# Routed feed-forward network in items of up to 512 rows, with gate and up sums in banks of their own

## Chip, core and metric

The kernel runs on one core of one Trainium2 chip, as one program of several stages that follow each other with a barrier between them. The metric is the device time of one execution in microseconds (us); lower is better. The median of three runs of the kernel before is 2126.97 us (2122.52 to 2127.93).

## What is computed

Two layers over 2048 rows of 512 values. The change touches the feed-forward network of the first layer, in which each row goes to one of two experts:

```
logits = x @ gate_w.T
sel = argmax(softmax(logits)); top_w = probability of sel
g = einsum('td,efd->etf', x, w_gate)      # 2 experts, 2048 hidden features
u = einsum('td,efd->etf', x, w_up)
h = silu(g) * u
y = einsum('etf,edf->etd', h, w_down)
out = einsum('etd,te->td', y, onehot * top_w)
```

The kernel sorts the rows by expert and computes for each row its own expert alone. Every fp32 product is made of three matmuls on split operands (high x high, high x low, low x high; PASSES in the code), so every operand is held as a high part (a rounded copy) and a low part (the difference).

## The kernel before

The function is routed_ffn_stage. The 2048 sorted rows and 128 spare ones are 17 tiles of 128 rows. The weights of one 128-feature slice of an expert are one `w` buffer of 1536 columns: four chunks of 256 (128 gate, 128 up) and 512 of down. The 16 slices (RG) are 16 passes over all 17 tiles; two passes are one turn of a hardware loop, and the first and last two stand outside of it. In a pass, five `w` buffers serve four blocks of 4, 2, 1 and 1 pairs of tiles (RBLOCKS) and the single last tile, since each block belongs to one expert that is known only at run time.

The unit of work is a step: one pair of tiles, 256 rows, nine steps in a pass (eight pairs, then the single tile). In a step:

- TensorE (`hidden_pair`, L745) sums gate and up of the pair into the two halves of one PSUM bank `hidden`: 2 x 4 chunks x 3 passes = 24 matmuls of 256 columns. Then come the down products of the pair before (`down`, L766): 2 tiles x 3 = 6 matmuls of 512 columns into two `y` banks. The single tile takes 12 matmuls of 256 columns (L754), 3 down matmuls and one transpose of `h32_single` (L790).
- ScalarE makes the silu of the gate half (L658), then the high part of h (L666).
- VectorE multiplies up by silu into the PSUM tile `h32` (L703), makes the low part of h (L706), and adds the two `y` banks of the pair before to `rows` (L692, a copy at L690 in the first pass).

The queues run in program order. TensorE waits for the low part of h before down (`s_h`), for the addition that frees the `y` bank (`s_yadd`), and for the weights of a block (`s_w`). A weight buffer is filled (`filled`) by a DMA of SyncE's queue into one of two `raw` buffers, a high copy on ScalarE (L642) and a subtraction on GpSimd (L621); ScalarE's copies of the five buffers are queued behind the high parts of steps 5, 7, 8, 0 and 1. The DMA of a buffer waits until the buffer two before it is finished.

In the first pass the rows come in as well: TensorE turns a tile (`turn_x`, L734, four transposes), ScalarE writes the high part (L646), VectorE the low part (L678). Tiles 0 to 3 are turned ahead of the steps, in four banks; the others go through one bank `x` one after the other, each turn waiting for the low part of the tile before (`s_x`). Two tiles enter in each step, one after the hidden sums and one after down, and they are those of two steps later (LEAD = 2).

Of the kernel before, what the change touches and what calls it, by code (L numbers as in the profile page):

```python
# [11 lines left out]
P = 128  # L12
D = 512
# [464 lines left out]
def routed_ffn_stage(nc, w_dram, xs_dram, ys_dram, ident_dram, keep):  # L478
# [10 lines left out]
    def halves(n):  # L489

        return RT * (n // RU) + 2 * (n % RU)

    with ExitStack() as ctx:
# [14 lines left out]
        enter_banks = [yb[t // 2][t % 2][:].rearrange("p (c r) -> p c r", c=KC) for t in range(4)]  # L508
# [20 lines left out]
        def bank_of(t):  # L529

            return enter_banks[t] if t < 2 * LEAD else turned[:]

# [7 lines left out]
        LEAD = 2  # L540

        def walk(i, first, step):

            for j in range(2):
                for u in range(RU):
                    n = RU * j + u
                    entering = (2 * (u + LEAD), 2 * (u + LEAD) + 1) if first and j == 0 else ()
                    step(2 * RU * i + n, 2 * RT * i, n, j, u, first and n == 0, [t for t in entering if t < RT])

        def filled(i, j, u, last, fill):  # L550
# [3 lines left out]
            if u in (5, 7, 8) and not (last and j == 1):  # L554
                fill(i, RB * (j + 1) + (5, 7, 8).index(u), False)
# [61 lines left out]
        def _(pool):  # L617
# [10 lines left out]
            def body(i, first, last):  # L628
                for j in range(2):
                    for u in range(RU):  # L630
                        filled(i, j, u, last, fill)
# [3 lines left out]
        def _(act):  # L635
# [13 lines left out]
            for t in range(2 * LEAD):  # L649
                x_high(t)  # L650

            def body(i, first, last):
                def step(k, k0, n, j, u, start, entering):
                    cols = slice(0, PR if u < RP else P)
                    act.wait_ge(s_hid, k + 1)
# [7 lines left out]
                    if not isinstance(k, int) or k >= 2:  # L663
                        act.wait_ge(s_y, k0 + halves(n - 1))
                    src = hp[:, n % 2, :] if u < RP else turned[:, 0, :]
# [2613 lines left out]
```

## Time and profile before

| | before |
|---|---|
| median of three runs | 2126.97 us |
| the profiled execution: its own time | 2123.35 us |
| the profiled execution: span of the trace | 2121.6 us |
| TensorE matmuls busy | 1803.0 us (85%), 10016 instructions |
| VectorE / ScalarE / GpSimd busy | 1231.4 / 848.3 / 1032.3 us |
| mean granted TensorE clock | 0.92 |
| the routed stage's steps on TensorE | about 100 to 703 us of the span |

Busy time is the time in which an engine has an instruction under way. Matmuls overlap, so their cost is read from start to start, not from their durations. A row of the timeline gives start, duration, engine, line, operation, output <- inputs, shapes, and in brackets the engine's idle time before it with what ended it. A row with a count higher than 1 merges neighbours. The granted clock is a share of full speed: 1.00 is 2.4 GHz, 0.50 is 1.2 GHz.

### The profile page before, as it was taken

The page shows a single profiled execution, that of the slowest core. Times are in us where ns is not written, and L with a number is a line of the kernel's source. Part 1 is how long each engine was busy: PE and PEld are TensorE (multiplying, and loading weights), DVE is VectorE, ACT ScalarE, POOL GpSimd, SP SyncE. Part 2 cuts the span into 40 slices and gives each one's busy share as a digit, 9 for nine tenths or more (in the row PEclk, how much of TensorE's full clock was granted, in tenths as well). Part 3 has the DMA queues.
Part 4 walks back from the last instruction along what each step waited for, and adds up shares of the span by engine and source line. Part 5 has one row for each costly group of instructions (what it writes and reads, how often), then busy time and mean ns, then how long its engine had stood idle before and what let it go on. Part 6 is the DMA issues. An engine that isn't in the chain of part 4 may idle for free. (4 is left out here: it accounts for less than half of the span.)

```text
span 2121.6 us, 29604 instructions
## 1 busy us (share of the span) xinstructions
PE 1803.0 (85%) x10016; PEld 1475.2 (70%) x10016; DVE 1231.4 (58%) x1916; ACT 848.3 (40%) x1426; POOL 1032.3 (49%) x654
## 2 busy tenths in 40 slices
PE   3389999999999688986669956765999999996996
PEld 2189999999999333432238845655999999995775
DVE  5244544444444579999606623662666666565886
ACT  3233333433333246455321211442666666661221
POOL 0325453545454245554312566213877777764564
PEclk7699999999999899998879977877999999998998
DMA  5634232323333400221680141103788778776564
GB/s 204 213 115 135 90 120 101 109 100 119 104 110 124 175 20 26 94 90 59 208 314 1 41 169 29 47 1 109 269 284 286 276 281 282 274 258 206 195 205 132
DMA packets 106858, 316.86 MB, mean 149 GB/s; under 512 B 14531, under 2 KB 16161, under 8 KB 105505
## 3 DMA queue, kind: packets, MB, share of 16 engines
q1 hardware_dynamic: 89536, 266.07, 36.5%
q0 software_dynamic: 17248, 49.86, 7.0%
q8 instruction: 40, 0.66, 0.1%
q14 instruction: 34, 0.27, 0.0%
HBM read 248.17 MB, written 67.71 MB: 149 GB/s over the span
## 5 line engine op out<-in xcount | busy, mean ns | idle before, releaser
L703 DVE TENSOR_TENSOR rffn_ps_h<-rffn_ps_hidden,rffn_silu 128x256 f32<-128x256 f32 x128 | 55.4, 432 | 234.3 <-ACT rffn_silu L658 234.3
L692 DVE TENSOR_TENSOR rows<-rffn_ps_y,rows 128x512 f32<-128x512 f32 x255 | 165.1, 681 | 2.5 <-PE rffn_ps_y L766 1.1
L745 PE MATMUL rffn_ps_hidden<-rffn_xsh,rffn_w0h 128*128 128x256 f32 x512 | 147.7, 288 | 0.0
L745 PE MATMUL rffn_ps_hidden<-rffn_xsl,rffn_w0h 128*128 128x256 f32 x512 | 146.0, 285 | 0.0
L745 PE MATMUL rffn_ps_hidden<-rffn_xsh,rffn_w0l 128*128 128x256 f32 x512 | 145.9, 285 | 0.0
L658 ACT ACTIVATE rffn_silu<-rffn_ps_hidden 128x256 f32<-128x256 f32 x144 | 53.3, 370 | 230.0 <-PE rffn_ps_hidden L745 226.6
L621 POOL TENSOR_TENSOR rffn_w0l<-rffn_raw,rffn_w0h 128x1536 fp32r<-128x1536 f32 x15 | 52.7, 3513 | 177.6 <-ACT rffn_w0h L642 177.6
L1873 POOL DMA_INDIRECT moe_x_in<-xn_rows,moe_idx_now x94 | 99.4, 1057 | 21.2 <-issue 14.7
L1879 POOL TENSOR_TENSOR moe_w_0l<-moe_raw,moe_w_0h 128x1536 fp32r<-128x1536 f32 x24 | 84.3, 3514 | 40.2 <-ACT moe_w_0h L1904 40.2
L745 PEld LDWEIGHTS rffn_ps_hidden<-rffn_xsh,rffn_w0h 128*128 128x128 f32 x512 | 99.2, 194 | 3.6 <-issue 0.3
L745 PEld LDWEIGHTS rffn_ps_hidden<-rffn_xsl,rffn_w0h 128*128 128x128 f32 x512 | 99.3, 194 | 1.8
L745 PEld LDWEIGHTS rffn_ps_hidden<-rffn_xsh,rffn_w0l 128*128 128x128 f32 x512 | 99.2, 194 | 0.0
L1946 DVE COPY moe_y<-moe_ps_y 128x512 f32<-128x512 f32 x94 | 64.4, 685 | 56.5 <-PE moe_ps_y L1987 53.7
L1879 POOL TENSOR_TENSOR moe_w_1l<-moe_raw,moe_w_1h 128x1536 fp32r<-128x1536 f32 x23 | 80.9, 3519 | 31.4 <-ACT moe_w_1h L1904 31.4
L621 POOL TENSOR_TENSOR rffn_w1l<-rffn_raw,rffn_w1h 128x1536 fp32r<-128x1536 f32 x15 | 52.8, 3517 | 74.8 <-ACT rffn_w1h L642 74.8
L2903 POOL DMA_INDIRECT att_rows<-ys,pos x64 | 66.9, 1046 | 39.7 <-POOLq L55 22.8
L1924 ACT ACTIVATE moe_h<-moe_ps_hidden,moe_b 128x256 f32<-128x256 f32 x141 | 64.2, 471 | 55.0 <-PE moe_ps_hidden L2004 54.0
L621 POOL TENSOR_TENSOR rffn_w3l<-rffn_raw,rffn_w3h 128x1536 fp32r<-128x1536 f32 x16 | 56.4, 3522 | 58.6 <-ACT rffn_w3h L642 58.6
L2004 PE MATMUL moe_ps_hidden<-moe_xs0h,moe_w_0h 128*128 128x256 f32 x288 | 81.5, 283 | 1.5 <-DVE moe_xs0l L1938 1.5
L2004 PE MATMUL moe_ps_hidden<-moe_xs0h,moe_w_0l 128*128 128x256 f32 x288 | 81.6, 283 | 0.0
L2004 PE MATMUL moe_ps_hidden<-moe_xs0l,moe_w_0h 128*128 128x256 f32 x288 | 81.3, 282 | 0.0
L1428 PE MATMUL mix_ps_k<-mix_mix,mix_w 128*128 128x512 f32 x128 | 62.0, 631 | 20.7 <-DVE mix_mix L1114 17.1
(710 smaller groups left out, 6352.5 us busy)
## 6 DMA issues: line engine op xcount, KB each, us to landing
rffn_raw<-in_ffn_w SPq DMA_DIRECT2D x80, 768.0 KB, 4.3
moe_raw<-in_moe_w SPq DMA_DIRECT2D x47, 769.5 KB, 4.3
moe_raw<-in_moe_w SPq DMA_DIRECT2D x47, 768.0 KB, 5.2
ys<-moe_y SPq DMA_DIRECT2D x47, 512.0 KB, 3.0
xs<-route_zero SPq DMA_DIRECT2D x17, 256.0 KB
rffn_x_in<-xs SPq DMA_DIRECT2D x17, 256.0 KB, 2.7
ys<-rows SPq DMA_DIRECT2D x17, 256.0 KB, 2.1
rows<-in_x SPq DMA_DIRECT2D x4, 1024.0 KB, 9.0
```

The costliest lines, as they stand in the source:

```text
L621: nc.gpsimd.tensor_tensor(w[b][LO][:], raw[m % 2][:], f32(w[b][HI][:]), ALU.subtract).then_inc(s_w, 1)
L658: nc.scalar.activation(sil[n % 2][:, cols], hb[n % 2][:, 0, cols], ACT.Silu).then_inc(s_sil, 1)
L692: nc.vector.tensor_tensor(y[:, 2 * u + tt, :], yb[n % 2][tt][:], y[:, 2 * u + tt, :], ALU.add)\
L703: nc.vector.tensor_tensor(hp[:, n % 2, :], hb[n % 2][:, 1, :], sil[n % 2][:], ALU.mult)\
L745: last = nc.tensor.matmul(hb[n % 2][:, half, :], wu[p][:, col:col + P], xs[q][:, c, u * PR:(u + 1) * PR], start=(c == 0 and m == 0), stop= ...
L1428: last = nc.tensor.matmul(bank[:], w[m][:, k, c * P:(c + 1) * P], mix[m][:, k, :], start=(k == 0), stop=(k == KC - 1))
L1873: nc.gpsimd.indirect_dma_start(out=x_in[j][tt][:], out_offset=None, in_=xn_dram, in_offset=bass.IndirectOffsetOnAxis(ap=now[j][:, tt:tt + ...
L1879: nc.gpsimd.tensor_tensor(w1[j][LO][:], raw1[j][:, 0:W1], f32(w1[j][HI][:]), ALU.subtract).then_inc(s_w1, 1)
L1924: nc.scalar.activation(h32[f][:], hb[f][:], ACT.Relu, bias=b1[j][:, f:f + 1]).then_inc(s_h32, 1)
L1946: nc.vector.tensor_copy(y[:, tt, :], yb[tt][:]).then_inc(s_yc, 1)
L2004: last = nc.tensor.matmul(hb[f][:], w1[j][p][:, col:col + P], xs[j][q][:, c, :], start=(c == 0 and n == 0), stop=(c == KC - 1 and n == 2))
L2903: nc.gpsimd.indirect_dma_start(out=rows[k % 2][s][:], out_offset=None, in_=ys_dram, in_offset=bass.IndirectOffsetOnAxis(ap=keep.pos4[:, s, ...
```

## The change

A pass is made of six items: three of 4 tiles (512 rows), two of 2 tiles, one single (ITEMS). The block of four pairs is items 0 and 1, the block of two pairs item 2, the two blocks of one pair items 3 and 4. Gate and up have separate banks (two of each, `gb` and `ub`), each up to 512 columns; there are two `y` banks in place of four, used in turn by tile; `h32` is one bank, no longer two halves.

On TensorE a step is now: gate of item n (12 matmuls), the first half of the down tiles of item n-1 ("ahead"), up of item n (12 matmuls), the second half of the down tiles of n-1 ("behind"). VectorE's order in a step: additions of the ahead tiles, the product, additions of the behind tiles, the low part of h. For the single tile the product stands first. ScalarE's silu waits for gate alone. The weight copies are queued behind the high parts of items 3, 4, 5 and of items 0 and 1 of the next pass.

In the first pass the tiles of item n+1 enter in step n: tiles 4 to 7 in step 0, 8 to 11 in step 1, two each in steps 2 and 3, one in step 4. Turns stand after gate, in the middle of up, after up, and after the behind tiles. The first item waits for four tiles.

```diff
+    QR = 4 * P
...
+    ITEMS = [4, 4, 4, 2, 2, 1]
+    NI = len(ITEMS)
+    START = [sum(ITEMS[:u]) for u in range(NI)]
+    ITEM_BLOCK = [BLOCK_OF[t // 2] for t in START]
+
+    def tiles(n):
+
+        return RT * (n // NI) + START[n % NI]
+
+    def sums(n):
+
+        return (2 * NI - 1) * (n // NI) + 2 * (n % NI)
...
-        sil = [a.sb(f"silu{i}", [P, PR]) for i in range(2)]
+        sil = [a.sb(f"silu{i}", [P, QR]) for i in range(2)]
-        hT = [[a.sb(f"hT{i}{'hl'[s]}", [P, PR], F32R) for s in (HI, LO)] for i in range(2)]
-        hb = [a.ps(f"hidden{i}", [P, 2, PR]) for i in range(2)]
-        yb = [[a.ps(f"y{i}{tt}", [P, D]) for tt in range(2)] for i in range(2)]
-        hp = a.ps("h32", [P, 2, PR])
+        hT = [[a.sb(f"hT{i}{'hl'[s]}", [P, QR], F32R) for s in (HI, LO)] for i in range(2)]
+        gb = [a.ps(f"gate{i}", [P, QR]) for i in range(2)]
+        ub = [a.ps(f"up{i}", [P, QR]) for i in range(2)]
+        yb = [a.ps(f"y{i}", [P, D]) for i in range(2)]
+        hp = a.ps("h32", [P, QR])
...
+                for u in range(NI):
+                    n = NI * j + u
+                    entering = list(range(START[u + 1], START[u + 1] + ITEMS[u + 1])) if first and j == 0 and u + 1 < NI else []
+                    step(2 * NI * i + n, n, j, u, first and n == 0, entering)
...
-            if u in (5, 7, 8) and not (last and j == 1):
-                fill(i, RB * (j + 1) + (5, 7, 8).index(u), False)
+            if u >= 3 and not (last and j == 1):
+                fill(i, RB * (j + 1) + u - 3, False)
...
-                    nc.scalar.activation(sil[n % 2][:, cols], hb[n % 2][:, 0, cols], ACT.Silu).then_inc(s_sil, 1)
-                    if u < RP:
+                    nc.scalar.activation(sil[n % 2][:, cols], gb[n % 2][:, cols], ACT.Silu).then_inc(s_sil, 1)
+                    for t in entering[:3]:
+                        x_high(t)
...
-                    src = hp[:, n % 2, :] if u < RP else turned[:, 0, :]
+                        act.wait_ge(s_y, 2 * RT * i + tiles(n - 1))
+                    src = hp[:, cols] if ITEMS[u] > 1 else turned[:, 0, :]
                     nc.scalar.copy(hT[n % 2][HI][:, cols], src).then_inc(s_hhi, 1)
-                    for t in entering:
+                    for t in entering[3:]:
...
+                for tt in parts:
+                    g, t = tiles(n) + tt, START[n % NI] + tt
+                    dve.wait_ge(s_y, 2 * RT * i + g + 1)
...
+                    cols = slice(0, ITEMS[u] * P)
+                    prior = [] if start else list(range(ITEMS[(u - 1) % NI]))
+                    ahead, behind = prior[:(len(prior) + 1) // 2], prior[(len(prior) + 1) // 2:]
+                    fresh = first and n <= NI
...
+                    def enter(e):
+                        if e < len(entering):
+                            x_low(entering[e])
...
+                    def product():
+                        dve.wait_ge(s_hid, 2 * (2 * NI - 1) * i + sums(n) + (2 if ITEMS[u] > 1 else 1))
+                        dve.wait_ge(s_sil, k + 1)
                         if not start:
                             dve.wait_ge(s_hhi, k)
-                        nc.vector.tensor_tensor(hp[:, n % 2, :], hb[n % 2][:, 1, :], sil[n % 2][:], ALU.mult)\
...
+                        if ITEMS[u] > 1:
+                            nc.vector.tensor_tensor(hp[:, cols], ub[n % 2][:, cols], sil[n % 2][:, cols], ALU.mult)\
+                              .then_inc(s_h32, 1)
...
+                    if ITEMS[u] == 1:
+                        product()
+                    enter(0)
+                    add(i, n - 1, ahead, fresh)
+                    enter(1)
+                    if ITEMS[u] > 1:
+                        product()
+                    enter(2)
+                    add(i, n - 1, behind, fresh)
+                    enter(3)
+                    dve.wait_ge(s_hhi, k + 1)
+                    src = hp[:, cols] if ITEMS[u] > 1 else turned[:, 0, :]
+                    nc.vector.tensor_tensor(hT[n % 2][LO][:, cols], src, f32(hT[n % 2][HI][:, cols]), ALU.subtract)\
+                      .then_inc(s_h, 1)
...
-            def hidden_pair(n, u):
-                wu = w[BLOCK_OF[u]]
-                for half in range(2):
-                    for c in range(KC):
...
+            def half(n, u, bank, side, steps, sem=True):
+
+                wu, cols = w[ITEM_BLOCK[u]], ITEMS[u] * P
+                rows = slice(START[u] * P, START[u] * P + cols)
+                for c in steps:
+                    col = c * GU + side * P
+                    for m, (p, q) in enumerate(PASSES):
+                        last = nc.tensor.matmul(bank[n % 2][:, 0:cols], wu[p][:, col:col + P], xs[q][:, c, rows],
+                                                start=(c == 0 and m == 0), stop=(c == KC - 1 and m == 2))
+                if steps[-1] == KC - 1:
+                    last.then_inc(s_hid, 1)
...
+            def down(i, k, n, parts):
+                if parts:
+                    wu = w[ITEM_BLOCK[n % NI]]
+                    pe.wait_ge(s_h, k + 1)
+                for tt in parts:
+                    g = tiles(n) + tt
+                    if not isinstance(i, int) or 2 * RT * i + g >= 2:
+                        pe.wait_ge(s_yadd, 2 * RT * i + g - 1)
                     for m, (p, q) in enumerate(PASSES):
-                        last = nc.tensor.matmul(yb[n % 2][tt][:], hT[n % 2][p][:, tt * P:(tt + 1) * P],
+                        last = nc.tensor.matmul(yb[g % 2][:], hT[n % 2][p][:, tt * P:(tt + 1) * P],
                                                 wu[q][:, DOWN:RW], start=(m == 0), stop=(m == 2))
                     last.then_inc(s_y, 1)
...
+                def step(k, n, j, u, start, entering):
+                    prior = [] if start else list(range(ITEMS[(u - 1) % NI]))
+                    ahead, behind = prior[:(len(prior) + 1) // 2], prior[(len(prior) + 1) // 2:]
...
                     if first and j == 0:
-                        pe.wait_ge(s_x, min(2 * u + 2, RT))
...
+                    if START[u] // 2 in FIRST_OF:
+                        pe.wait_ge(s_w, 2 * RB * i + RB * j + ITEM_BLOCK[u] + 1)
                     if not isinstance(k, int) or k >= 2:
                         pe.wait_ge(s_h32, k - 1)
-                    if u < RP:
-                        hidden_pair(n, u)
+                    if ITEMS[u] > 1:
+                        half(n, u, gb, 0, range(KC))
+                        enter(0)
+                        down(i, k - 1, n - 1, ahead)
+                        half(n, u, ub, 1, range(0, KC // 2))
+                        enter(1)
+                        half(n, u, ub, 1, range(KC // 2, KC))
+                        enter(2)
+                        down(i, k - 1, n - 1, behind)
+                        enter(3)
                     else:
                         hidden_single(n)
-                    if entering:
-                        turn_x(entering[0])
-                    if not start:
-                        down(k - 1, k0, n - 1, (u - 1) % RU)
-                    if len(entering) > 1:
-                        turn_x(entering[1])
-                    if u == RP:
+                        down(i, k - 1, n - 1, ahead + behind)
                         pe.wait_ge(s_h32, k + 1)
                         nc.tensor.transpose(turned[:, 0, :], single[:], ident[:]).then_inc(s_T, 1)
                 walk(i, first, step)
             pairs(pe, body)
-            down(RG * RU - 1, 2 * RT * (RG // 2 - 1), 2 * RU - 1, RP)
+            down(RG // 2 - 1, RG * NI - 1, 2 * NI - 1, [0])
```

## Rows read from the trace of the kernel before

**Rows 1.** Busy time by stretch, ten and more passes, then one: engines, clock, DMA.
```profile
core 0: us, PE busy (x) PEld busy (x) DVE busy (x) ACT busy (x) POOL busy (x), PEclk, DMA share, GB/s
150.00:700.00 550.00, 550.00 (x3877) 515.89 (x3876) 268.26 (x531) 201.84 (x347) 259.30 (x74) 1.00 0.34 111
156.03:192.36 36.33, 36.33 (x259) 34.09 (x257) 17.69 (x36) 13.47 (x23) 17.53 (x6) 1.00 0.34 110
```
**Rows 2.** Line L790, once a pass: min/median/max ns, first and last start.
```profile
L790 PE MATMUL rffn_ps_x<-rffn_ident,rffn_h_single x16: 270/270/270, 156.0 to 701.0; 128*128 128x128 f32 x16
```
**Rows 3.** Timeline of TensorE: first of 24 hidden sums, first of 6 down, next.
```profile
305.00 0.28 PE L745 MATMUL rffn_ps_hidden<-rffn_xsh,rffn_w0h 128*128 128x256 f32 x1
...
307.87 0.40 PE L766 MATMUL rffn_ps_y<-rffn_w0h,rffn_hT1h 128*128 128x512 f32 x1
...
309.25 0.28 PE L745 MATMUL rffn_ps_hidden<-rffn_xsh,rffn_w0h 128*128 128x256 f32 x1
```
**Rows 4.** Timeline of TensorE, shared experts: hidden matmuls of 512 columns, 1st and 29th.
```profile
1193.49 0.39 PE L285 MATMUL shared_ps_hid<-xn1h,shared_w1h 128*128 128x512 f32 x1
...
1199.83 0.39 PE L285 MATMUL shared_ps_hid<-xn1l,shared_w1h 128*128 128x512 f32 x1
```
**Rows 5.** Timeline of one steady step: ScalarE and VectorE after the hidden sums.
```profile
316.38 0.40 PE L766 MATMUL rffn_ps_y<-rffn_w0h,rffn_hT1h 128*128 128x512 f32 x1
316.58 0.38 ACT L658 ACTIVATE rffn_silu<-rffn_ps_hidden 128x256 f32<-128x256 f32 x1 [2.10 <-PE rffn_ps_hidden L745]
317.00 0.43 DVE L703 TENSOR_TENSOR rffn_ps_h<-rffn_ps_hidden,rffn_silu 128x256 f32<-128x256 f32 x1 [0.87 <-ACT rffn_silu L658]
317.54 0.37 ACT L666 CAST rffn_hT0h<-rffn_ps_h 128x256 fp32r<-128x256 f32 x1 [0.57 <-DVE rffn_ps_h L703]
317.94 0.42 DVE L706 TENSOR_TENSOR rffn_hT0l<-rffn_ps_h,rffn_hT0h 128x256 fp32r<-128x256 f32 x1 [0.51 <-ACT rffn_hT0h L666]
318.29 1.28 DVE L692 TENSOR_TENSOR rows<-rffn_ps_y,rows 128x512 f32<-128x512 f32 x2
```
**Rows 6.** Timeline, end of the stage: what TensorE loses at a wait for h.
```profile
701.79 0.28 DVE L719 TENSOR_TENSOR rffn_hT1l<-rffn_ps_x,rffn_hT1h 128x128 fp32r<-128x128 f32 x1
702.12 0.50 PE L766 MATMUL rffn_ps_y<-rffn_w4h,rffn_hT1h 128*128 128x512 f32 x1 [0.87 <-DVE rffn_hT1l L719]
702.46 0.39 PE L766 MATMUL rffn_ps_y<-rffn_w4l,rffn_hT1h 128*128 128x512 f32 x1
```
**Rows 7.** Timeline of GpSimd, SyncE's queue and ScalarE: how the weights are filled.
```profile
336.41 3.51 POOL L621 TENSOR_TENSOR rffn_w1l<-rffn_raw,rffn_w1h 128x1536 fp32r<-128x1536 f32 x1 [5.00 <-ACT rffn_w1h L642]
340.09 3.81 SPq L591 DMA_DIRECT2D rffn_raw<-in_ffn_w  x2
344.41 1.48 ACT L642 CAST rffn_w3h<-rffn_raw 128x1536 fp32r<-128x1536 f32 x1 [2.12 <-DMA rffn_raw<-in_ffn_w]
```
**Rows 8.** Timeline, entry of the first pass: turns of x and first sums.
```profile
104.13 0.56 PE L745 MATMUL rffn_ps_hidden<-rffn_xsh,rffn_w0h 128*128 128x256 f32 x1
105.13 0.69 DVE L678 TENSOR_TENSOR rffn_xsl<-rffn_ps_y,rffn_xsh 128x512 fp32r<-128x512 f32 x1 [0.16 <-ACT rffn_xsh L646]
...
111.57 1.08 PE L734 MATMUL rffn_ps_x<-rffn_ident,rffn_x_in 128*128 128x128 f32 x4 [2.21 <-DVE rffn_xsl L678]
...
119.16 0.63 PE L734 MATMUL rffn_ps_x<-rffn_ident,rffn_x_in 128*128 128x128 f32 x4 [0.82 <-DVE rffn_xsl L678]
119.54 0.36 PE L745 MATMUL rffn_ps_hidden<-rffn_xsh,rffn_w0h 128*128 128x256 f32 x1
119.82 0.59 ACT L646 CAST rffn_xsh<-rffn_ps_x 128x512 fp32r<-128x512 f32 x1 [1.54 <-PE rffn_ps_x L734]
120.44 0.69 DVE L678 TENSOR_TENSOR rffn_xsl<-rffn_ps_x,rffn_xsh 128x512 fp32r<-128x512 f32 x1 [0.24 <-ACT rffn_xsh L646]
```
**Rows 9.** Busy time by stretch, entry (columns as in Rows 1): the granted clock.
```profile
107.94:111.35 3.41, 1.42 (x12) 1.18 (x11) 1.47 (x3) 1.24 (x3) 0.00 (x0) 1.00 0.69 232
111.35:114.77 3.42, 3.20 (x15) 3.23 (x16) 0.77 (x2) 1.96 (x2) 0.00 (x0) 0.50 0.34 94
```

More of the change, by code:

```diff
@@ L629, in body @@
                 for j in range(2):
-                    for u in range(RU):
+                    for u in range(NI):
                         filled(i, j, u, last, fill)
@@ L682, in _, with add @@
                 nc.vector.tensor_tensor(w[m][LO][:], raw[m % 2][:], f32(w[m][HI][:]), ALU.subtract).then_inc(s_w, 1)
-            for t in range(2 * LEAD):
+            for t in range(ITEMS[0]):
                 x_low(t)
-            def add(k0, n, u, fresh=False):
-                for tt in range(2 if u < RP else 1):
-                    dve.wait_ge(s_y, k0 + halves(n) + tt + 1)
+            def add(i, n, parts, fresh):
+                for tt in parts:
+                    g, t = tiles(n) + tt, START[n % NI] + tt
+                    dve.wait_ge(s_y, 2 * RT * i + g + 1)
@@ L689, in add @@
                     if fresh:
[L690 removed]
+                        nc.vector.tensor_copy(y[:, t, :], yb[g % 2][:]).then_inc(s_yadd, 1)
                     else:
[L692 to L693 removed]
+                        nc.vector.tensor_tensor(y[:, t, :], yb[g % 2][:], y[:, t, :], ALU.add).then_inc(s_yadd, 1)
@@ L695, in body, with step @@
             def body(i, first, last):
-                def step(k, k0, n, j, u, start, entering):
-                    cols = slice(0, PR if u < RP else P)
-                    dve.wait_ge(s_sil, k + 1)
-                    fresh = first and n <= RU
-                    if u < RP:
+                def step(k, n, j, u, start, entering):
+                    cols = slice(0, ITEMS[u] * P)
+                    prior = [] if start else list(range(ITEMS[(u - 1) % NI]))
[7 more added lines that the diff above has]
+                        dve.wait_ge(s_sil, k + 1)
@@ L721, in body @@
                 walk(i, first, step)
             pairs(dve, body)
-            add(2 * RT * (RG // 2 - 1), 2 * RU - 1, RP)
+            add(RG // 2 - 1, 2 * NI - 1, [0], False)
         @block.tensor
@@ L735, in turn_x @@
                 last.then_inc(s_xt, 1)
-            for t in range(2 * LEAD):
+            for t in range(ITEMS[0]):
                 turn_x(t)
-            def hidden_pair(n, u):
-                wu = w[BLOCK_OF[u]]
-                for half in range(2):
-                    for c in range(KC):
-                        col = c * GU + half * P
-                        for m, (p, q) in enumerate(PASSES):
-                            last = nc.tensor.matmul(hb[n % 2][:, half, :], wu[p][:, col:col + P],
-                                                    xs[q][:, c, u * PR:(u + 1) * PR],
-                                                    start=(c == 0 and m == 0), stop=(c == KC - 1 and m == 2))
-                last.then_inc(s_hid, 1)
+            def half(n, u, bank, side, steps, sem=True):
[8 more added lines that the diff above has]
+                    last.then_inc(s_hid, 1)
             def hidden_single(n):
@@ L753, in hidden_single @@
                     for m, (p, q) in enumerate(PASSES):
-                        last = nc.tensor.matmul(hb[n % 2][:, 0, :], xs[p][:, c, RP * PR:RP * PR + P],
+                        last = nc.tensor.matmul(gb[n % 2][:, 0:GU], xs[p][:, c, RP * PR:RP * PR + P],
                                                 wu[q][:, c * GU:(c + 1) * GU],
```

59 lines of the change are left out of this document (14 added, 45 removed).

## The prediction

> **What bounds the kernel now.** I read the page first: TensorE has a matmul under way for 85% of the span, so the question is whether the stage that changes is one in which TensorE never rests. The busy time by stretch answers it: from 150 to 700 us TensorE is busy for 550.00 of 550.00 us at a granted clock of 1.00, VectorE for 49%, ScalarE for 37%, GpSimd for 47% [rows 1]. One pass takes 36.33 us, read twice: as a stretch [rows 1], and as (701.0 - 156.0) / 15 from the transpose that comes once a pass [rows 2]. So in the steady passes only two things count: the start-to-start times of TensorE's instructions, and waits that the new order puts into its queue. The first pass is another case: it runs from about 104 to 156 us, with waits and a clock that falls [rows 8, 9].
>
> The price of a matmul is read from start to start. 24 hidden matmuls of 256 columns take 307.87 - 305.00 = 2.87 us, 0.120 each; 6 down matmuls of 512 columns take 309.25 - 307.87 = 1.38 us, 0.230 each [rows 3]. In the shared experts 28 hidden matmuls of 512 columns, built like the new ones, take 1199.83 - 1193.49 = 6.34 us, 0.2264 each [rows 4]. A pass then adds up: 192 x 0.120 + 12 x 0.120 for the single + 51 x 0.230 = 23.0 + 1.4 + 11.7 = 36.2, of 36.33 measured.
>
> **Wide hidden matmuls.** Items 0 to 2 hold six of the eight pairs: 144 matmuls of 256 columns become 72 of 512, 17.28 us of them per pass. No row shows a wide hidden matmul in this stage, with its traffic from VectorE and ScalarE. Bounds: 0.2264 (same shape, quieter stage [rows 4]) gives 16.30 and a gain of 0.98 us; 0.240, twice a narrow one, gives nothing. The down matmuls of this very stage, 0.230 [rows 3], stand between, and I take 0.229: 16.49 us, a gain of 0.79 us per pass. Down, single item, transpose and the weight fills keep their number; of the instruction kinds on ScalarE and VectorE each does the same columns in fewer instructions, and both engines have half their time free [rows 1].
>
> The Trainium skill (TensorE: Matmul & The Clock Gate, "Wait — 56ns, not 53.3ns?") speaks against the change: warm back-to-back matmuls start N / 2.4 GHz + about 2.5 ns apart, that is 0.1092 and 0.2158 us for 256 and 512 columns. The rows differ: 0.120 and 0.226 to 0.230. By the page the edit would save 72 x 2.5 ns = 0.18 us per pass; its effect is the second rival's.
>
> **The new waits of a steady pass.** Call U the moment at which TensorE goes on after up of item n. Silu starts 0.20 us after the hidden sums end (316.58 against 316.38) [rows 5]; now up decides, so the product starts at U + 0.20, and an addition 0.20 after its down tile. Durations at 512 columns: 0.59 on ScalarE and 0.69 on VectorE as for the parts of x [rows 8], 0.68 an addition; at 256 columns 0.43, 0.37, 0.42 [rows 5]. A down tile is 0.69 us (3 x 0.230).
>
> Item 2 is the tightest: four tiles of item 1 stand behind and ahead of it, and the gate after it is narrow. Product U + 0.20 to 0.89; high part to 1.52; additions of the two behind tiles 0.90 to 1.58 and, after the second tile ends at 1.38, 1.59 to 2.27; low part to 2.93, TensorE at 2.98 (0.05 after a low part [rows 6]). TensorE gets there at 1.38 + 12 x 0.120 = U + 2.82. It waits 0.16, and the first down matmul after a wait takes 0.34 instead of 0.23 to the next start [rows 6]: 0.27 us. What is queued behind this wait is the rest of TensorE's pass. For item 3 the same chain ends at 2.27 + 0.39 + 0.05 = 2.71 against 2.82, for item 4 (one tile behind) at about 2.0 against 0.69 + 1.44 = 2.13; the weight load is a slot ahead of its matmul, so I add 0.03. Items 0 and 1 have a wide gate after them (2.75 us): 2.26 against 2.75, and 2.98 against 4.13. The single item's product waits for ScalarE, which makes a weight copy of 1.48 us after item 4's high part: 1.05 + 1.48 + 0.28 + 0.3 = U4 + 3.2, against the transpose at 2.13 + 1.38 = 3.5. Two y banks in place of four cost nothing by this reckoning: the tile before last has been added at least one half of an item earlier. Sum of the waits: 0.30 us per pass, from 0 (the additions come 0.2 sooner) to 0.6.
>
> **Weight fills.** The copies move to later places. Item 3's high part ends at about 28.3 us of a pass of 35.8; the copy ends at 29.8, GpSimd's subtraction (3.51 [rows 7]) at 33.4, and TensorE wants block 0 at 35.8: 2.4 us to spare. The subtractions of the next two buffers end at 38.3 and 41.8, their DMAs' successors land 4.3 us behind (344.41 against 340.09 [rows 7]), at 42.8 and 46.3, and ScalarE asks for them at 43.5 and about 52. So ScalarE's present waits for these DMAs (2.12 us [rows 7]) go; they were hidden, and save nothing.
>
> **The first pass.** Gain of the wide matmuls 0.8, wait 0.3, as above. Item 0 needs tiles 2 and 3: it starts after the low part that ends at 105.82 instead of at 104.13 [rows 8], 1.8 us later. Before, TensorE waited 2.8 us around the turn at 111.57 (3.55 us for two turns that take 0.38 each at full clock), then five times for 0.8 us [rows 8] and a restart, 5.3: 8.1 us. After, a tile's chain from turn to turn is 0.66 + 0.62 + 0.69 + 0.15 = 2.1 us (119.16, 119.82, 120.44 [rows 8]). In step 0: turn 5 waits 0.45, turn 6 0.4, turn 7 1.75 (ScalarE and VectorE put the high part and the product in between), item 1 another 1.7; in step 1: 0.35, 0.4 and 1.8; in steps 2 and 3 0.4, because a tile's low part now stands ahead of the product. Sum 7.2 + 1.8 = 9.0. Clock: it was 1.00 only from 107.94 on and fell back to 0.50 at 111.35 after 1.42 us busy of 3.41 [rows 9]; at 0.50 a narrow matmul costs 0.094 more, 29 of them 2.7 us. After: 12 wide ones at 0.427 instead of 0.229, 2.4 us, and as TensorE works for 1.0 of 3.4 us at the end of step 0, a fall with some 5 to 12 wide ones at 0.427, 1.0 to 2.4. In all 8.1 + 2.7 + 0.5 - 9.0 - 3.4 (to 4.8) = -1.1 to -2.5 us; if the clock is up at 107.94 as before and never falls, 5 at 0.427 cost 1.0 and the sum is +1.3. I take -1.0, the mild end of the likelier case.
>
> **Sum.** Fifteen steady passes x (0.79 - 0.30) = 7.4 us, first pass -1.0, together 6.4. The profiled execution took 2123.35 us, so 2117.0; it lies 3.6 us below the median of the runs shown, and the same step from 2126.97 gives **2120.6 us**. A measurement of this kernel can tell about 0.3%, 6.4 us, from no change; the forecast lies on that border.
>
> **Rivals.** (1) Forecast, 50%: 2116 to 2124. (2) The wide matmul saves little, 15%: what lies above 0.107 us per 256 columns is this stage's traffic and grows with the columns. At 0.236 the gain of 0.29 is eaten by the waits: 2128. Against it stand 0.230 and 0.2264 [rows 3, 4]; by the skill's 2.5 ns, 0.18 - 0.30 = -0.12 per pass, 2129.8. (3) Slower, 15%: the handover of h is late. Each 0.1 us that the chain of product, additions and low part is longer costs 0.1 at item 2 at once, and at items 3 and 4 from 0.12 on. Beyond about +0.25 us the gain is gone; at +0.4 (a product of 512 columns into PSUM at 1.1 us, which no row shows at that width) the waits are 0.30 + 0.4 + 2 x 0.3 = 1.3 per pass, 0.5 more than the gain: 15 x 0.5 = 7.5 us, 1.0 of the entry, 2135.5. For it: three items within 0.16 us of their need. Against: 0.43 for 256 into PSUM is hardly more than 0.42 into SBUF [rows 5]. (4) The entry stays at 0.50 into step 2, 10%: some 30 more wide matmuls at 0.427, 30 x 0.2 = 6 us, 2126.6. (5) More than forecast, 10%: 0.2264 per wide matmul, waits of 0.1, entry +1.3: 15 x 0.88 + 1.3 = 14.5, 2112.5. That the change doesn't do what it says I hold for excluded: the widths stand in the code.
>
> **Range.** From 2110 to 2131: cases 1, 2, 4 and 5 with 1.5 us of measurement below, and a part of 3; some 15 in 100 lie outside. Faster by over 0.3%: all of 5 and somewhat over half of 1, 0.38. Within 0.3%: the rest of 1, nearly all of 2 and 4, a little of 3, 0.47. Slower by more: most of 3, 0.15.
>
> **What will show it.** Right: the single item's transposes 35.85 us apart instead of 36.33; wide hidden matmuls 0.229 apart; TensorE idle once a pass, for about 0.2 us, before the first down of item 2, released by VectorE's low part; the second pass starting near 157 us. Wrong, if wide matmuls are 0.235 or more apart, if such waits stand at items 3, 4 or the single too, if TensorE waits for weights at item 0, or if the clock is 0.50 after 125 us.

## The result and the profile after

| | before | after |
|---|---|---|
| median of twelve runs each | 2125.86 us (2118.55 to 2128.05) | 2117.72 us (2111.00 to 2123.72) |
| ratio | | 0.9967, 95% interval 0.9954 to 0.9980 |
| span of the trace | 2121.6 us | 2115.8 us |
| matmuls | 10016 | 8864 |
| a steady pass | 36.33 us | 35.73 us |

The change takes 8.1 us (4.3 to 9.8 by the interval) off, where 6.4 were forecast. Twelve later runs of the same kernel, beside others of the kernel before, gave 0.9976 (0.9962 to 0.9989), 5.1 us (2.3 to 8.1).

Line L822 of the kernel after is the single item's transpose, once a pass, and answers to [rows 2]; the columns are min/median/max ns, first and last start. (690.6 - 154.6) / 15 = 35.73 us.

```profile
L822 PE MATMUL rffn_ps_x<-rffn_ident,rffn_h_single x16: 270/272/275, 154.6 to 690.6; 128*128 128x128 f32 x16
```

The busy time by stretch of the kernel after, columns as in [rows 1]:

```profile
160.00:690.00 530.00, 529.28 (x2735) 450.38 (x2734) 257.16 (x431) 180.18 (x250) 254.43 (x73) 1.00 0.34 113
```

TensorE is still busy at full clock, but 0.72 us are missing now, and by the overlap of the records a gap between starts is longer than the idle time shown. In the timelines PE is TensorE's matmuls, DVE VectorE, ACT ScalarE, PEld TensorE's loads. The starts of the wide matmuls, which [rows 3] answer to, are read from TensorE's timeline in the kernel after:

```profile
236.10 0.39 PE L767 MATMUL rffn_ps_up<-rffn_xsh,rffn_w0h 128*128 128x512 f32 x1
236.33 0.39 PE L767 MATMUL rffn_ps_up<-rffn_xsl,rffn_w0h 128*128 128x512 f32 x1
...
238.82 0.39 PE L790 MATMUL rffn_ps_y<-rffn_w0h,rffn_hT0h 128*128 128x512 f32 x1
...
240.18 0.39 PE L767 MATMUL rffn_ps_gate<-rffn_xsh,rffn_w1h 128*128 128x512 f32 x1
```

Twelve wide ones take 238.82 - 236.10 = 2.72 us, 0.2267 each. That is the price of the quieter shared experts [rows 4], and not one between it and the 0.230 of the down matmuls in [rows 3]. The six down matmuls here take 1.36, 0.227 each too.

The wait that the prediction put at item 2 stands there, in every steady pass (0.19 us late, 0.11 in the last two). The timeline of the kernel after, from the end of up of item 2 (U = 246.98, the start of the first down matmul behind) to the first down matmul of item 2:

```profile
247.34 0.70 DVE L723 TENSOR_TENSOR rffn_ps_h<-rffn_ps_up,rffn_silu 128x512 f32<-128x512 f32 x1 [2.19 <-PE rffn_ps_up L767]
247.95 1.28 DVE L704 TENSOR_TENSOR rows<-rffn_ps_y,rows 128x512 f32<-128x512 f32 x2
248.15 0.59 ACT L677 CAST rffn_hT0h<-rffn_ps_h 128x512 fp32r<-128x512 f32 x1 [4.45 <-DVE rffn_ps_h L723]
249.15 0.68 DVE L740 TENSOR_TENSOR rffn_hT0l<-rffn_ps_h,rffn_hT0h 128x512 fp32r<-128x512 f32 x1
249.65 0.28 PE L767 MATMUL rffn_ps_gate<-rffn_xsh,rffn_w2l 128*128 128x256 f32 x1
249.96 0.49 PE L790 MATMUL rffn_ps_y<-rffn_w1h,rffn_hT0h 128*128 128x512 f32 x1
250.29 0.40 PE L790 MATMUL rffn_ps_y<-rffn_w1l,rffn_hT0h 128*128 128x512 f32 x1
```

The low part ends at 249.83, U + 2.85, and down starts at U + 2.98. The narrow gate would have let it start at 249.77: 0.19 us late, and the next start follows 0.33 later instead of 0.23. Together 0.29 us; the prediction had 0.27 and U + 2.98.

A second gap was not predicted. In the same kernel, where one turn of the hardware loop ends, behind the single item:

```profile
260.74 0.28 ACT L667 ACTIVATE rffn_silu<-rffn_ps_gate 128x128 f32<-128x128 f32 x1
261.04 0.29 DVE L726 TENSOR_TENSOR rffn_h_single<-rffn_ps_gate,rffn_silu 128x128 f32<-128x128 f32 x1 [1.13 <-ACT rffn_silu L667]
261.30 0.40 PE L790 MATMUL rffn_ps_y<-rffn_w3h,rffn_hT0l 128*128 128x512 f32 x1
261.54 0.27 PE L822 MATMUL rffn_ps_x<-rffn_ident,rffn_h_single 128*128 128x128 f32 x1
261.97 0.49 PE L767 MATMUL rffn_ps_gate<-rffn_xsh,rffn_w0h 128*128 128x512 f32 x1 [0.16 <-issue]
```

The transpose is followed 0.43 us later by the next gate instead of 0.03. Such a gap stands at the end of five turns of the loop: 0.43 us here, where the product of the single item ends 0.21 us before the transpose starts (261.33 against 261.54), and 0.32 to 0.33 us at the other four, where it ends 0.28 to 0.29 us before. From the second of them on, passes last 35.61 and 35.95 us in turn. In the passes between, in the middle of a turn, the product ends 0.39 us before and the gate follows at 0.03. In the kernel before it ends 0.59 us before, and the gate follows after 0.02 to 0.07 us everywhere.

In this one pass the down product of item 4 starts late too (260.05 instead of 259.96, and the next start follows 0.33 later), 0.19 us that no other steady pass of this profile shows.

### The profile page after: what moved, and what is told of

Its sections match the earlier page's. It is cut to its first block and busy times, and to the rows that moved or that the text cites. A ratio compares the mean times of both kernels' runs of the same rounds, so it can differ in the third digit from the quotient of the medians.

```text
span 2115.8 us, 27097 instructions
## 1 busy us (share of the span) xinstructions
PE 1791.7 (85%) x8864; PEld 1412.2 (67%) x8864; DVE 1228.9 (58%) x1820; ACT 830.0 (39%) x1330; POOL 1033.7 (49%) x654
## 5 line engine op out<-in xcount | busy, mean ns | idle before, releaser
L704 DVE TENSOR_TENSOR rows<-rffn_ps_y,rows 128x512 f32<-128x512 f32 x255 | 172.9, 690 | 126.2 <-PE rffn_ps_y L790 124.1
L723 DVE TENSOR_TENSOR rffn_ps_h<-rffn_ps_up,rffn_silu 128x512 f32<-128x512 f32 (+1 forms) x80 | 47.4, 593 | 124.3 <-PE rffn_ps_up L767 124.0
L677 ACT CAST rffn_hT0h<-rffn_ps_h 128x512 fp32r<-128x512 f32 (+1 forms) x48 | 24.8, 516 | 155.8 <-DVE rffn_ps_h L723 141.1
L630 POOL TENSOR_TENSOR rffn_w4l<-rffn_raw,rffn_w4h 128x1536 fp32r<-128x1536 f32 x16 | 56.1, 3507 | 59.6 <-ACT rffn_w4h L651 59.6
L1985 DVE TENSOR_TENSOR moe_w_0l<-moe_raw,moe_w_0h 128x1536 fp32r<-128x1536 f32 x24 | 59.0, 2457 | 43.2 <-ACT moe_w_0h L1950 43.2
L630 POOL TENSOR_TENSOR rffn_w3l<-rffn_raw,rffn_w3h 128x1536 fp32r<-128x1536 f32 x16 | 56.1, 3506 | 55.6 <-ACT rffn_w3h L651 55.6
L1985 DVE TENSOR_TENSOR moe_w_1l<-moe_raw,moe_w_1h 128x1536 fp32r<-128x1536 f32 x23 | 51.5, 2241 | 50.6 <-ACT moe_w_1h L1950 47.5
L2036 PE MATMUL moe_ps_hidden<-moe_xs1h,moe_w_1h 128*128 128x256 f32 x276 | 77.4, 280 | 2.5 <-issue 2.5
L2036 PE MATMUL moe_ps_hidden<-moe_xs1h,moe_w_1l 128*128 128x256 f32 x276 | 77.3, 280 | 0.0
L2036 PE MATMUL moe_ps_hidden<-moe_xs1l,moe_w_1h 128*128 128x256 f32 x276 | 77.0, 279 | 0.0
L1526 PE MATMUL mix_ps_ro<-mix_w,mix_wkv 128*128 128x512 f32 x128 | 62.5, 644 | 16.2 <-POOL mix_wkv L1074 14.9
```

Of the source, the lines that this page charges most:

```text
L630: nc.gpsimd.tensor_tensor(w[b][LO][:], raw[m % 2][:], f32(w[b][HI][:]), ALU.subtract).then_inc(s_w, 1)
L704: nc.vector.tensor_tensor(y[:, t, :], yb[g % 2][:], y[:, t, :], ALU.add).then_inc(s_yadd, 1)
L723: nc.vector.tensor_tensor(hp[:, cols], ub[n % 2][:, cols], sil[n % 2][:, cols], ALU.mult)\
L1526: last = nc.tensor.matmul(ro[t % 2][:], wkv[b % 2][:, k, t * P:(t + 1) * P], w[O_][:, k, :], start=(k == 0), stop=(k == KC - 1))
L1985: nc.vector.tensor_tensor(w2[j][LO][:], raw2[:], f32(w2[j][HI][:]), ALU.subtract).then_inc(s_w2, 1)
L2036: last = nc.tensor.matmul(hb[f][:], w1[j][p][:, col:col + P], xs[j][q][:, c, :], start=(c == 0 and n == 0), stop=(c == KC - 1 and n == 2))
```

## The experiments

All kernels but two are the changed one with the edit shown. Ratios are to the kernel before, on the same chip. The medians are from four comparisons, in which the kernel before had 2125.86 us (after), 2121.39 (the wide matmuls as two of 256, the first two edits and both), 2121.10 (the kernel before again, x through the y banks, all three, four of 128) and 2124.01 (the runs "again" of the others), so a median is compared only within its group. The pass is read from the single item's transpose, as above.

| kernel | ratio (95% interval) | median us | pass us | first turn to first transpose of the single, us |
|---|---|---|---|---|
| before | | | 36.33 | 56.0 |
| before, again | one run | 2124.83 | 36.33 | 55.2 |
| after | 0.9967 (0.9954 to 0.9980) | 2117.72 | 35.73 | 53.6 |
| after, again | 0.9976 (0.9962 to 0.9989) | 2118.89 | 35.74 | 55.8 |
| wide matmuls as two of 256 | 1.0027 (1.0012 to 1.0042) | 2130.07 | 36.73 | 59.8 |
| low part between the additions | 0.9965 (0.9948 to 0.9982) | 2114.27 | 35.46 | 54.6 |
| weight copy behind the silu | 0.9966 (0.9952 to 0.9979) | 2113.55 | 35.63 | 54.8 |
| both | 0.9952 (0.9934 to 0.9970) | 2111.95 | 35.35 | 54.9 |
| both, again | 0.9947 (0.9930 to 0.9964) | 2112.05 | 35.34 | 58.0 |
| x through the y banks | 0.9965 (0.9947 to 0.9982) | 2115.68 | 35.75 | 55.2 |
| all three | 0.9930 (0.9905 to 0.9955) | 2110.43 | 35.35 | 54.8 |
| all three, again | 0.9945 (0.9926 to 0.9963) | 2108.93 | 35.33 | 50.9 |
| wide matmuls as four of 128 | one run | 2384.46 | 51.65 | 89.5 |

**Is the width the gain?**

```diff
-                for c in steps:
+                pieces = [cols * steps[0] // KC + v for v in range(0, cols * len(steps) // KC, 256)] if cols > PR else [0]
+                for v in pieces:
+                    width = 256 if cols > PR else cols
+                    for c in (range(KC) if cols > PR else steps):
...
-                        last = nc.tensor.matmul(bank[n % 2][:, 0:cols], wu[p][:, col:col + P], xs[q][:, c, rows],
+                            last = nc.tensor.matmul(bank[n % 2][:, v:v + width], wu[p][:, col:col + P],
+                                                    xs[q][:, c, START[u] * P + v:START[u] * P + v + width],
```

Of a wide up sum, the left 256 columns are summed in the first half and the right 256 in the second. The kernel with four of 128 has 128 in place of 256 in both lines.

> The changed kernel with its order, banks and waits, but each wide hidden matmul (512 columns) issued as two of 256 columns, first all chunks of the left 256, then of the right. Theory (each matmul has a cost of its own of some 13 ns above its columns, so the width is where the gain comes from): 72 x 0.2267 us become 144 x 0.120 us in a pass, the pass grows by 0.96 from 35.73 to 36.7 us and the kernel by 15.4 us against the changed one, to about 2133 us, slower than the kernel before by the waits that the new order adds. Rival (the order and banks gave the gain, the width little; by the Trainium skill, TensorE: Matmul & The Clock Gate, the fixed part is 2.5 ns a matmul): the pass grows by 0.2 us, the kernel by 3 us, to 2121 us.

The transpose line of this kernel:

```profile
L826 PE MATMUL rffn_ps_x<-rffn_ident,rffn_h_single x16: 270/272/276, 159.2 to 710.2; 128*128 128x128 f32 x16
```

551.0 / 15 = 36.73 us: 1.00 more than after, where 0.96 was expected and 0.2 by the rival. At the width of the kernel before, the new order costs 0.40 us per pass, and the kernel is slower than the one before, 1.0027. The width is all of the gain in the steady passes; the order is its price. What the width stands for is two things at once: half as many matmuls, and half as many loads of a stationary operand (LDWEIGHTS), since each matmul has its own (10016 of both in the kernel before, 8864 of both after). No run separates them.

**What is the price of a width made of?**

> The changed kernel with each wide hidden matmul issued as four of 128 columns (72 of 512 become 288 of 128 in a pass). If the price of a matmul is its columns at 2.4 GHz plus a fixed 13 ns at any width, 288 x 0.067 = 19.2 us, passes of 38.6 us, 2164 us. If under some width the load of the stationary operand sets the distance, as the 0.107 us of the 128-column matmuls in the attention's scores suggests, 288 x 0.10 = 28.8 us, passes of 48.2 us, about 2318 us.

Both numbers missed: passes of 51.65 us. TensorE's timeline in the kernel with pieces of 128 columns, half of an up sum (48 matmuls) and the down product after it:

```profile
311.12 0.22 PE L770 MATMUL rffn_ps_up<-rffn_xsh,rffn_w0h 128*128 128x128 f32 x1
...
315.98 0.28 PE L770 MATMUL rffn_ps_up<-rffn_xsh,rffn_w0l 128*128 128x128 f32 x1
...
316.43 0.45 PE L794 MATMUL rffn_ps_y<-rffn_w0h,rffn_hT0h 128*128 128x512 f32 x1
```

48 matmuls in 316.43 - 311.12 = 5.31 us, 0.1106 each. That is hardly less than the 0.120 for 256 columns. So the second theory fits, a floor under the distance of two such matmuls, with 0.1106 and not the 0.10 put in. The attention's scores had shown this number already: ten distances from 1980.00 to 1981.11 us in the kernel before are 0.111 each, not the 0.107 of the expectation. 288 x 0.1106 - 72 x 0.2267 = 15.5 us, of 15.9 measured.

That the load of the stationary operand (PEld) is this floor is supported by the start of the same sum:

```profile
311.12 0.19 PEld L770 LDWEIGHTS rffn_ps_up<-rffn_xsl,rffn_w0h 128*128 128x128 f32 x1
311.18 0.27 PE L770 MATMUL rffn_ps_up<-rffn_xsl,rffn_w0h 128*128 128x128 f32 x1
311.23 0.19 PEld L770 LDWEIGHTS rffn_ps_up<-rffn_xsh,rffn_w0l 128*128 128x128 f32 x1
311.29 0.28 PE L770 MATMUL rffn_ps_up<-rffn_xsh,rffn_w0l 128*128 128x128 f32 x1
```

The first matmul, whose operand had been loaded during the down product before, is followed 0.06 us later by the second (311.12, 311.18); from then on each matmul starts 0.06 us behind its own load, and the loads start 0.11 us apart. So the columns alone need no more than 0.06. A run in which two matmuls share a load would test it, and there is none.

Above the floor the price is 13 ns over the columns at 2.4 GHz at both widths (0.120 - 0.1067, 0.2267 - 0.2133). The 2.5 ns that the Trainium skill gives (TensorE: Matmul & The Clock Gate, "Wait — 56ns, not 53.3ns?") are not what these three-pass products on fp32 operands pay.

**The wait at item 2.**

```diff
                     enter(2)
-                    add(i, n - 1, behind, fresh)
-                    enter(3)
+                    add(i, n - 1, behind[:1], fresh)
                     dve.wait_ge(s_hhi, k + 1)
                     src = hp[:, cols] if ITEMS[u] > 1 else turned[:, 0, :]
                     nc.vector.tensor_tensor(hT[n % 2][LO][:, cols], src, f32(hT[n % 2][HI][:, cols]), ALU.subtract)\
                       .then_inc(s_h, 1)
+                    add(i, n - 1, behind[1:], fresh)
+                    enter(3)
```

> The changed kernel with one edit on VectorE: where two tiles stand behind, the low part of h stands between their two additions and no longer after both. Theory (the wait of TensorE before the first down product of item 2 is the queue order on VectorE): the low part of item 2 ends at U + 2.27 instead of U + 2.85, the wait and the restart of 0.27 us per pass vanish, the pass goes from 35.73 to 35.46 us, the kernel gets 4 us faster than the changed one. Rival (the wait is there for the y bank that the second addition frees, since there are two banks only): the wait moves to the second down tile and the pass stays at 35.7.

The same stretch of item 2 in this kernel, one pass, with U = 245.97:

```profile
246.94 0.68 DVE L704 TENSOR_TENSOR rows<-rffn_ps_y,rows 128x512 f32<-128x512 f32 x1
247.14 0.59 ACT L677 CAST rffn_hT0h<-rffn_ps_h 128x512 fp32r<-128x512 f32 x1 [4.45 <-DVE rffn_ps_h L723]
247.76 0.69 DVE L739 TENSOR_TENSOR rffn_hT0l<-rffn_ps_h,rffn_hT0h 128x512 fp32r<-128x512 f32 x1
248.37 0.68 DVE L704 TENSOR_TENSOR rows<-rffn_ps_y,rows 128x512 f32<-128x512 f32 x1
248.77 0.40 PE L791 MATMUL rffn_ps_y<-rffn_w1h,rffn_hT0h 128*128 128x512 f32 x1
249.00 0.40 PE L791 MATMUL rffn_ps_y<-rffn_w1l,rffn_hT0h 128*128 128x512 f32 x1
```

The low part ends at 248.45, U + 2.48 (the high part, U + 1.76, is what holds it now; 2.27 had been expected). Down starts at U + 2.80 and goes on 0.23 later: no wait, and the two y banks are no limit. The pass is 35.46 us, the number expected. The time of the whole kernel does not show this edit alone, nor the next: 0.9965 and 0.9966 against the 0.9967 and 0.9976 of the changed kernel.

**The gap at the end of a loop turn.**

```diff
                     nc.scalar.activation(sil[n % 2][:, cols], gb[n % 2][:, cols], ACT.Silu).then_inc(s_sil, 1)
+                    if u == 5 and not (last and j == 1):
+                        fill(i, RB * (j + 1) + 1, False)
...
-                    filled(i, j, u, last, fill)
+                    if u != 4:
+                        filled(i, j, u, last, fill)
```

> The changed kernel with one edit on ScalarE: the weight copy of block 1 stands behind the silu of the single item, no longer ahead of it. Theory (the product of the single item comes just too late for its transpose, because the copy of 1.48 us holds its silu, and so TensorE's queue has nothing left with which to cover the end of a turn of the hardware loop): the gap of 0.32 to 0.43 us behind the transpose, in every second pass, goes to 0.03; pass pairs take 71.27 instead of 71.6 us; seven turns, 2.3 us for the kernel. Rival (the larger loop body costs its time at the turn whatever waits): pass pairs stay at 71.6 us.

The end of a loop turn in this kernel:

```profile
261.12 0.28 ACT L667 ACTIVATE rffn_silu<-rffn_ps_gate 128x128 f32<-128x128 f32 x1 [0.70 <-PE rffn_ps_gate L779]
261.29 1.47 ACT L651 CAST rffn_w1h<-rffn_raw 128x1536 fp32r<-128x1536 f32 x1
261.43 0.29 DVE L729 TENSOR_TENSOR rffn_h_single<-rffn_ps_gate,rffn_silu 128x128 f32<-128x128 f32 x1 [0.55 <-ACT rffn_silu L667]
262.50 0.27 PE L825 MATMUL rffn_ps_x<-rffn_ident,rffn_h_single 128*128 128x128 f32 x1
262.52 0.48 PE L770 MATMUL rffn_ps_gate<-rffn_xsh,rffn_w0h 128*128 128x512 f32 x1
```

The product ends 0.78 us before the transpose instead of 0.21 (0.60 to 0.62 at the other turns), and the gate follows 0.02 us after it (at most 0.05). The passes no longer alternate: 35.63 in the mean, 35.50 to 35.83. That is 1.6 us for the kernel, five gaps and not the seven expected (2.3 us). A larger loop body alone costs nothing visible, since this one is as large. So the gap needs both, the end of a turn and a product that is only just in time; what TensorE's queue does there, the trace does not show.

> Both edits at once, the low part of h between the additions behind, and the copy of block 1 behind the single item's silu. Theory: both gains add, 4 + 2.3 us, passes of 35.35 us, about 2111.5 us. Rival: either one was covering the other, or a new wait takes its place, and the sum is no more than the larger one, 4 us.

Passes of 35.35 us: the two gains add (0.27 + 0.10 = 0.37, measured 0.38). The median, 2111.95, meets the expected 2111.5 by luck: in this comparison the kernel before had 2121.39, 4.5 us less than in the first. The second run:

> The changed kernel with the low part between the additions behind and the copy of block 1 behind the single item's silu, with more runs, on the chip of the changed one. 15 x (35.74 - 35.34) = 6 us faster than the changed kernel, ratio to the kernel before about 0.993; if the stages behind swallow it, 0.995.

35.34 us, as expected, and 0.9947, where 0.993 or 0.995 had been given. Against the changed kernel beside it, it is 6.8 us faster in the medians, with 6 expected; what moved is the changed kernel's own ratio, 0.9976 instead of 0.9967.

**The first pass.** It is read from the first turn of x to the first transpose of the single item.

> The kernel before once more, for a second profile. If the 2.4 us that the changed kernel's first pass was shorter (53.6 instead of 56.0 us from the first turn to the single item's transpose) come from its order, this run shows 56 us again, within 0.5. If they come from where the clock happens to rise, it shows anything from 54 to 58. The stages behind the routed one take 1417.7 us in the first profile; by both theories they vary by some us from run to run, which explains that the spans differ by less than the routed stage.

55.2 us, 0.8 less than in the first profile: more than the 0.5 that the first theory allowed, and within the 54 to 58 of the second.

> The changed kernel once more, with more runs and a second profile of its own first pass. Steady passes 35.74 us again. From the first turn to the single item's transpose: if the order of the first pass is worth something of its own, 54 to 55 us again, as in three runs with the same order (54.6, 54.8, 54.9), against 55.3 and 56.0 of the kernel before; if 53.6 against 56.0 was the clock's rise alone, it can as well be 56. Ratio to the kernel before 0.996.

55.8 us, so the 53.6 of the first profile was not the order. Five runs with the changed kernel's order gave 53.6, 54.6, 54.8, 54.9 and 55.8, and one 58.0. This is the one with 58.0 (both edits, again), its busy time by stretch, columns as in [rows 1], the clock the third from the right:

```profile
101.80:111.57 9.77, 8.03 (x25) 6.07 (x26) 2.77 (x4) 3.63 (x5) 0.00 (x0) 0.50 0.90 306
111.57:121.90 10.33, 7.18 (x37) 5.15 (x37) 4.06 (x6) 4.70 (x7) 0.35 (x1) 1.00 0.42 118
121.90:125.30 3.40, 3.40 (x10) 2.53 (x9) 0.00 (x0) 0.00 (x0) 3.10 (x1) 0.50 0.02 5
125.30:135.50 10.20, 8.33 (x43) 6.32 (x42) 6.36 (x10) 4.70 (x7) 0.15 (x1) 1.00 0.35 99
135.50:138.90 3.40, 3.40 (x9) 2.66 (x8) 0.00 (x0) 0.00 (x0) 3.31 (x1) 0.50 0.03 11
```

The clock came up only at 111.57 and fell twice, each time behind a stretch in which TensorE had waited for x (busy for 7.18 of 10.33 us, and for 8.33 of 10.20). In the kernel after it was up from 104.06 to 117.71, fell once, and the pass was 4.4 us shorter.

The edit for these waits, tiles 5 and 6 of x turned into the two y banks:

```diff
-            return enter_banks[t] if t < ITEMS[0] else turned[:]
+            return enter_banks[t] if t < ITEMS[0] else enter_banks[t - 5] if t in (5, 6) else turned[:]
...
-                if t > ITEMS[0]:
+                if t > 7:
                     pe.wait_ge(s_x, t)
+                elif t == 7:
+                    pe.wait_ge(s_x, 5)
```

> The changed kernel with one edit in the first pass: tiles 5 and 6 are turned into the two y banks, which are free until step 1, instead of the one bank x, so that turns 5, 6 and 7 no longer wait for the low part of the tile before. Theory (at the entry TensorE waits for the chain turn, high part, low part through the one bank): the waits at turns 5 and 6 (0.4 each) and at turn 7 (1.5) go, item 1 still waits for the low part of tile 7, and the entry gets 1.5 to 2.5 us shorter than the 53.6 to 54.9 us of the runs with the order of the changed kernel. Rival (item 1 waits for the low part of tile 7 whenever the turns come, since ScalarE and VectorE make the parts one after the other): under 0.7 us. Steady passes 35.74 by both.

The waits went: item 1 starts 118.31 - 111.68 = 6.6 us after the end of item 0's gate, against 117.41 - 108.99 = 8.4 in the kernel after. But the first pass took 55.2 us, not the 51 to 53 expected. Against the 53.6 of the kernel after, the 1.8 us are there, and two losses stand ahead of the edited place: item 0 started 6.2 us after the first turn instead of 5.1, since x arrived later, and its gate ran at the lower clock level almost throughout and took 111.68 - 106.43 = 5.25 us instead of 108.99 - 106.09 = 2.90. In item 1's gate the lower level stood in both. The kernel's ratio, 0.9965, does not tell the edit from the changed kernel.

> The three edits together: low part between the additions behind, copy of block 1 behind the single item's silu, tiles 5 and 6 turned into the y banks. Theory: passes of 35.34 us as with the first two, and what the entry edit gives alone on top: 6 + 2 us faster than the changed kernel, about 0.993 of the kernel before. Rival: the entry edit is lost in the noise of the clock's rise, 0.995.

Passes of 35.35 us and 0.9930, as expected, but from four runs only, and the first pass took 54.8 us.

> The same with tiles 5 and 6 turned into the y banks. Item 1 starts 6.6 us after the end of item 0's gate instead of 8.4, so 1.8 us faster than with the two edits alone wherever the clock stays up: ratio 0.992. If a shorter wait only lets the clock fall at another place, the ratio is that of the two edits, 0.993, and the first pass takes 54 to 55 us as in the others.

The expected 0.992 did not come: 0.9945 (0.9926 to 0.9963). In this profile 6.9 us from gate to item 1, and the clock stayed up:

```profile
101.93:105.30 3.37, 3.32 (x14) 2.58 (x15) 1.38 (x2) 1.41 (x3) 0.00 (x0) 0.50 0.96 315
105.30:110.04 4.74, 3.34 (x16) 2.56 (x15) 1.38 (x2) 2.21 (x3) 0.00 (x0) 1.00 0.99 365
110.04:116.90 6.86, 4.70 (x30) 3.84 (x28) 3.97 (x6) 4.22 (x7) 0.00 (x0) 1.00 0.56 183
116.90:152.79 35.89, 34.02 (x193) 28.78 (x193) 19.55 (x33) 13.16 (x22) 10.51 (x3) 1.00 0.29 94
```

50.9 us, the shortest first pass of all. The ratios of all three edits, 0.9930 and 0.9945, and of the two, 0.9952 and 0.9947, overlap: what the third is worth beyond the two stays open. The version with the two edits is shown in its passes (35.35 us). Both versions beat the changed kernel in the second comparison, by 6.8 us in the medians (2112.05 against 2118.89) and by 10.0 (2108.93); 6 were expected of the two.

## Why the prediction was right

**Size.** 8.1 us measured, 6.4 forecast, 2117.7 against 2120.6; the comparison repeated gave 5.1. The mechanism held: wide matmuls save, and the new order gives back a part at item 2. That the total came so near is partly luck. Both terms of the steady pass were too small, the gain by 0.17 us and the waits by 0.10, and the first pass and the stages behind move by more from run to run than lies between 6.4 and either measurement.

- **Wide matmuls.** Forecast 0.229 and a gain of 0.79 us per pass; measured 0.2267, that is 17.28 - 16.32 = 0.96, and 1.00 by the kernel with two of 256. The step that fell short is the choice between the bounds: I took the neighbouring down matmuls' price for the traffic of the stage. The lower bound, the same shape in another stage [rows 4], was the right row. Rival 2 falls with it. The 0.18 us per pass that the prediction worked out from the 2.5 ns of the Trainium skill (TensorE: Matmul & The Clock Gate, "Wait — 56ns, not 53.3ns?") falls too; the measurement is 1.00.
- **Waits.** Forecast 0.30 us per pass, 0.27 of it at item 2. Measured 0.40 (36.73 - 36.33, same widths). Item 2 is right to 0.02 us and was shown by taking it away (0.27). The rest is the gap at the loop's end, 0.11 per pass in the mean, which the prediction put at nothing: it held the single item's product to be 0.3 us early for its transpose (U4 + 3.2 against 3.5), which is what the traces show (0.28 to 0.29), but it did not ask whether that is enough at the end of a loop turn.
- **Steady passes together.** 0.60 us each instead of 0.49: 9.0 us for fifteen, not 7.4. Of the signs named, the transposes came 35.73 us apart (35.85), the wait at item 2 stands as described, the second pass started at 154.6 us (157), and none of the signs of being wrong showed, save that the gap at the loop's end stands behind the single item.
- **Weight fills** cost TensorE nothing, as reckoned, save through the copy ahead of the single item's silu, which makes the product just in time.
- **First pass.** Forecast 1.0 us longer. The waits of step 0 and 1 were right (in step 0, turns 5 and 6 came 0.42 and 0.37 us later than one turn and six wide matmuls behind the turn before, item 1 3.4 us later than two turns behind turn 6; 0.45, 0.4 and 3.45 forecast). Two terms were off: item 0 started 5.1 us after the first turn, against 4.2 and 5.3 in the two profiles of the kernel before, so the 1.8 us for tiles 2 and 3 was within what the arrival of x moves anyway; and the lower clock level took 1.7 us from wide matmuls in that profile (nine of item 1's gate, 121.16 - 117.41 us), not 3.4, since item 0 started with the clock up. In nine profiles the first pass of orders like the changed one took 50.9 to 58.0 us, and of the kernel before 55.2 and 56.0: a term of 1 us can't be told from it. The six profiles with exactly this first pass give 55.3 in the mean, the two before 55.6, so a first pass 1.0 longer is neither confirmed nor refuted.
- **Rivals.** The slower one (the handover at items 3 and 4) did not happen: the product of 512 columns into PSUM took 0.70 us, 0.69 assumed. Items 3 and 4 went on without a wait in the steady passes but one. Rival 5 had the right price of the wide matmul, and waits of 0.1 where 0.40 came. Something like rival 4 came in one profile (both edits, again): a clock at 0.50 for two stretches of 3.4 us, the second until 138.90 us.

**Where the rest went.** The routed stage's last addition starts at 692.8 us instead of 703.1, 10.3 us earlier, but the spans differ by 5.8. The stages behind it, which the change does not touch, took 1422.3 us in this profile and 1417.7 in the one before; in the second profile of each it was 1425.7 and 1420.3, over all the others 1415.2 to 1427.3. So one profile of each can't give the kernel's gain to better than some 5 us, and the medians of twelve runs give 8.1 and 5.1. The 9.0 us of the steady passes lie above both. Whether the change makes the stages behind it slower, or their own variation swallowed the rest, stays open.

## What to carry to other kernels

Where TensorE is never idle, price a matmul from start to start at each width: here everything above the columns at full clock was a fixed 13 ns per matmul at 256 and 512 columns, so halving the number at twice the width gained 6% of their time, and at 128 columns a floor made a matmul nearly as dear as one of 256. The order that makes room for the wide sums has to be costed queue by queue; a short item behind a long one is where the handover is tight, and splitting a pair of additions around the urgent step took the wait away for nothing. Ahead of the end of a hardware loop, look that the last thing TensorE waits for is there well before its turn: 0.2 to 0.3 us was too little here, 0.6 was enough. And where one stage varies by several us from execution to execution, as the first pass did (50.9 to 58.0 us), compare the steady passes and not one profile's span.

## What the runs showed of the hardware that I had not expected

- The distance of two fp32-split matmuls that each load their stationary operand is 0.111 us at 128 columns, against 0.120 at 256 and 0.227 at 512; at the start of such a sum one pair of 128 columns stood 0.06 apart, so it is not the columns that set the 0.111.
- At the end of a turn of the hardware loop TensorE goes on after 0.02 to 0.07 us where the product for its last instruction ended 0.59 us or more before that instruction's start, and after 0.32 to 0.43 us where it ended 0.21 to 0.29 us before. In the middle of a turn, 0.39 us before cost nothing (0.03).
- The first gap behind the single item's transpose is 0.31 to 0.33 us instead of 0.227 whatever waits (262.52 to 262.84 in the kernel with the later copy): the first wide matmul behind a transpose costs 0.09 us that no order here took away. A narrow one had 0.20 instead of 0.12. Behind down products the distance is 0.23 (240.18 to 240.41 in the kernel after).
